# Decoder layer with mixture of experts: router logits as dot products on VectorE, experts split in order

## The reference, cut to what matters

```
x = x + self_attention(norm(x))              # causal, 16 heads of 32
x = x + cross_attention(norm(x), ctx)        # one head of 512; keys and values: 256 of ctx and 256 of norm(x) through wk, wv
x = x + ffn(norm(x))                         # 8 experts, top 1

ffn:  logits = xt @ wg                       # (2048 x 512) @ (512 x 8)
      probs = softmax(logits); idx = argmax(probs); gate = probs[idx]
      out = gate * (xt @ W[idx].T + b[idx])  # each expert's W is 512 x 512
```

## Time and profile before

| what | us |
|---|---|
| median of 3 runs | 755.86 (754.78 to 756.69) |
| profiled execution, its own time | 756.65 |
| its span, first to last instruction | 754.9 |
| TensorE busy in the span | 679.7 |
| VectorE busy | 502.1 |
| ScalarE, GpSimd busy | 309.3, 327.8 |
| mean granted TensorE clock | 0.963 |

### The profile page before, as it was taken

The page is one execution under the profiler, slowest core; times in us unless marked ns, Lnnn a source line. Parts: engine busy times, 40 slices in busy tenths (PEclk is TensorE's granted clock), DMA queues, the critical chain, the costliest instruction groups (busy, mean ns, idle before and its releaser), DMA issues.

```text
span 754.9 us, 18988 instructions
## 1 busy us (share of the span) xinstructions
PE 679.7 (90%) x6040; PEld 604.4 (80%) x6041; DVE 502.1 (67%) x1479; ACT 309.3 (41%) x985; POOL 327.8 (43%) x559
## 2 busy tenths in 40 slices
PE   4768999999999989899999999999999983779994
PEld 4658798989898878778899999989898973658883
DVE  4667788888887878754647474747474649665663
ACT  3445565656666666633132323232323344112220
POOL 4376757575756686823301010100101258345652
PEclk9889999999999999999999999999999997679997
DMA  6487875656556656837813434352422282676520
GB/s 250 136 166 117 131 148 111 149 116 145 137 124 142 124 124 124 185 61 252 296 53 105 59 102 63 98 68 87 80 83 56 78 173 57 224 139 198 167 98 14
DMA packets 142745, 95.10 MB, mean 126 GB/s; under 512 B 110702, under 2 KB 114926, under 8 KB 142576
## 3 DMA queue, kind: packets, MB, share of 16 engines
q1 hardware_dynamic: 137040, 82.00, 46.6%
q0 software_dynamic: 5664, 12.61, 6.1%
HBM read 56.14 MB, written 18.77 MB: 99 GB/s over the span
## 4 chain that ended last, share of the span: by engine, by line
PE 44%; DVE 4%; DMA 3%; POOL 2%; issue 1%; ACT 0%; SPq 0%; POOLq 0%; DVEq 0%
PE b_bank L61 38%; PE b_bank L1462 2%; PE b_bank L1410 2%; DMA stage<-x2n,k_gather_no 2%; DVE k_at L975 1%; PE b_bank L1787 1%; DMA bias_sb<-in_wo 1%; PE b_bank L1434 1%; POOL w_lo L1294 1%; DVE w_lo L1094 0%; POOL w_hi L1292 0%; DVE x_sb L1534 0%; DVE b_stats L1579 0%; DVE w_lo L1507 0%; POOL slots L889 0%
## 5 line engine op out<-in xcount | busy, mean ns | idle before, releaser
L509 ACT ACTIVATE prob<-prob,shift 128x128 f32<-128x128 f32 (+1 forms) x256 | 114.6, 449 | 116.5 <-POOL shift L420 116.1
L1337 ACT CAST w_hi<-b_bank 128x256 fp32r<-128x256 f32 (+1 forms) x128 | 55.0, 447 | 153.7 <-PE b_bank L61 133.1
L61 PE MATMUL b_bank<-w_hi 128*128 128x256 f32 (+1 forms) x528 | 106.5, 324 | 3.2 <-DVE w_lo L1507 3.2
L61 PE MATMUL a_job<-w_hi 128*128 128x256 f32 (+1 forms) x488 | 95.0, 318 | 15.5 <-DVE w_lo L712 7.2
L61 PE MATMUL b_bank<-w_lo,w_hi 128*128 128x256 f32 (+1 forms) x528 | 103.8, 319 | 0.0
L61 PE MATMUL b_bank<-w_hi,w_lo 128*128 128x256 f32 (+1 forms) x528 | 103.7, 319 | 0.0
L733 DVE CUSTOM_DVE_ANT_0 prob<-a_s,mask 128x128 f32<-128x128 f32 (+1 forms) x256 | 79.7, 347 | 30.1 <-PE a_s L609 30.0
L1507 DVE TENSOR_TENSOR w_lo<-b_bank,w_hi 128x256 fp32r<-128x256 f32 (+1 forms) x128 | 61.4, 510 | 47.9 <-ACT w_hi L1337 47.4
L61 PEld LDWEIGHTS a_job<-w_hi 128*128 128x128 f32 x488 | 71.7, 197 | 25.3 <-DVE w_lo L712 7.8
L61 PE MATMUL a_job<-w_lo,w_hi 128*128 128x256 f32 (+1 forms) x488 | 88.0, 304 | 0.0
L61 PEld LDWEIGHTS b_bank<-w_hi 128*128 128x128 f32 x528 | 80.3, 191 | 9.5 <-DVE w_lo L1507 3.6
(11 more groups left out here) (185 smaller groups left out, 1136.7 us busy)
## 6 DMA issues: line engine op xcount, KB each, us to landing
stage<-in_w SPq DMA_DIRECT2D x6, 1024.0 KB, 10.4
xin<-in_x SPq DMA_DIRECT2D x8, 512.0 KB, 4.3
xr<-in_x SPq DMA_DIRECT2D x8, 512.0 KB, 4.1
x<-xr SPq DMA_DIRECT2D x8, 512.0 KB, 3.2
xin<-x SPq DMA_DIRECT2D x8, 512.0 KB, 8.6
stage<-in_ctx_t SPq DMA_DIRECT2D x8, 512.0 KB, 3.6
stage<-in_ctx SPq DMA_DIRECT2D x8, 512.0 KB, 3.5
xr<-x SPq DMA_DIRECT2D x8, 512.0 KB, 4.4
```

What stands on the lines that cost most here:

```text
L61: ins = pe_matmul(out, a, b, start=first and i == 0, stop=last and i == len(steps) - 1)
L509: a = nc.scalar.activation(prob[:, e % NPROB, cols], prob[:, e % NPROB, cols], ACT.Exp, scale=-1.0, bias=shift[:, e, q:q + 1], accum_out=r ...
L1337: nc.scalar.copy(hi, src).then_inc(job_hi, 1)
```

## The change

The logits of batches 0 to 6 are no longer made by Y0, Y1, l0 and l1, which leave `ORDER` (22 jobs are left). VectorE computes each as a fused multiply and sum over 512 channels of a row of `xn3_sb` with a row of `wg_t`, the transposed router matrix, which a new input brings and one DMA copies to all partitions, into the bias's tile. There are 16 per batch (8 experts, 2 tiles of tokens), dealt out behind jobs by two tables: `DOTS` (7 behind k1 to v1, 9 behind X1 to q2 of the next batch) and, for batch 6, `LAST_DOTS` (all behind k1 to v1). The last batch keeps TensorE's way.

The banks: jobs 0 to 13 take the seven banks twice, jobs 14 to 21 the last four twice. `ctx_t_lo` moves from s1 to y0.

The experts are split in the order 0 to 7 with one semaphore, each waiting for the one before. The buffers are dealt anew (`BUFFER`), with `xin` and `xn` as a fifth buffer; the output rows of the products move to `xr` and `prob`. GpSimd splits 0, 1 and 2 only (2 ahead of `next_tokens`), VectorE the rest: 3 and half of 4 between o0 and o3, `known_blocks` behind o3, the rest of 4, and 5, by the norm's steps, half of 6 behind `choose`, and half of 6 and all of 7 in the first four blocks of the products. A product waits only for its own expert. SP's loads, and the bias in two halves, follow the new buffers. `gates` gets a semaphore of its own and stands behind `place_tokens` in the last batch's first half; `STEPS` is 8. Scratch places 6 and 7 change names.

```diff
-        done = n * self.STEPS
         dve.wait_ge(self.ex_done, n + 1)
-        nc.vector.tensor_reduce(self.gsum[:], self.ex[:], AX.X, ALU.add).then_inc(self.step, 1)
-        dve.wait_ge(self.step, done + 5)
+        nc.vector.tensor_reduce(self.gsum[:], self.ex[:], AX.X, ALU.add).then_inc(self.gsum_done, 1)
+        dve.wait_ge(self.gsum_done, n + 1)
...
+        dve.wait_ge(self.step, done + 7)
+        nc.vector.tensor_reduce(self.slot[:], self.place[:], AX.X, ALU.add).then_inc(self.step, 1)
         dve.wait_ge(self.step, done + 8)
-        nc.vector.tensor_reduce(self.slot[:], self.place[:], AX.X, ALU.add).then_inc(self.step, 1)
-        dve.wait_ge(self.step, done + 9)
+        dve.wait_ge(self.token_done, n + 1)
         nc.vector.tensor_copy(self.slot_i[:], self.slot[:]).then_inc(self.slot_done, 1)
...
-    BUFFER = (0, 1, 4, 3, 2, 0, 2, 1)
-    HIGH_ORDER = (0, 1, 2, 4, 3, 5, 7, 6)
+    BUFFER = (0, 1, 0, 1, 2, 3, 4, 2)
...
+    def parts(self, e):
+        parts = self.stage[self.BUFFER[e]]
+        size = DC // len(parts)
+        return [(part, slice(i * size, (i + 1) * size)) for i, part in enumerate(parts)]
 
     def load(self, sp, w, e):
-        b = self.BUFFER[e]
-        wait(sp, self.split[b], self.earlier(e) * DC)
-        sp.dma_start(self.stage[b], w[e].rearrange("(c p) n -> p c n", p=P)).then_inc(self.loaded[b], 16)
+        if self.earlier(e):
+            self.wait_split(sp, self.earlier(e)[-1])
+        for part, chunks in self.parts(e):
+            sp.dma_start(part, w[e][chunks.start * P:chunks.stop * P, :].rearrange("(c p) n -> p c n", p=P))\
+                .then_inc(self.loaded[self.BUFFER[e]], 16)
 
     def high(self, nc, act, e):
-        act.wait_ge(self.loaded[self.BUFFER[e]], 16 * (self.earlier(e) + 1))
-        nc.scalar.copy(self.place(e)[0], self.stage[self.BUFFER[e]]).then_inc(self.hi_done, 1)
+        loads = sum(len(self.parts(i)) for i in self.earlier(e) + [e])
+        act.wait_ge(self.loaded[self.BUFFER[e]], 16 * loads)
+        for part, chunks in self.parts(e):
+            m = nc.scalar.copy(self.place(e)[0][:, chunks, :], part)
+        m.then_inc(self.hi_done, 1)
 
     def low(self, engine, e, pieces=range(DC)):
         hi, lo = self.place(e)
-        b = self.BUFFER[e]
-        engine.wait_ge(self.hi_done, self.HIGH_ORDER.index(e) + 1)
+        engine.wait_ge(self.hi_done, e + 1)
+        if e and pieces[0] == 0:
+            self.wait_split(engine, e - 1)
         for c in pieces:
-            engine.tensor_tensor(lo[:, c, :], self.stage[b][:, c, :], hi[:, c, :].bitcast(F32), ALU.subtract)\
-                .then_inc(self.split[b], 1)
+            part, chunks = next(p for p in self.parts(e) if c in range(p[1].start, p[1].stop))
+            engine.tensor_tensor(lo[:, c, :], part[:, c - chunks.start, :], hi[:, c, :].bitcast(F32), ALU.subtract)\
+                .then_inc(self.split, 1)
 
     def wait_split(self, engine, e):
-        engine.wait_ge(self.split[self.BUFFER[e]], DC * (self.earlier(e) + 1))
+        engine.wait_ge(self.split, e * DC + DC)
...
-        ORDER = ("X0 X1 s0 s1 q0 q1 p0 p1 q2 q3 o0 o1 o2 o3 k0 y0 y1 k1 k2 k3 v0 Y0 Y1 v1 l0 l1").split()
+        ORDER = ("X0 X1 s0 s1 q0 q1 p0 p1 q2 q3 o0 o1 o2 o3 k0 y0 y1 k1 k2 k3 v0 v1").split()
         FRONT = "Xqkv"
+        DOTS = {"k1": 1, "k2": 1, "k3": 1, "v0": 2, "v1": 2, "+X1": 2, "+s0": 2, "+s1": 1, "+q0": 1, "+q1": 1, "+p1": 1,
+                "+q2": 1}
+        LAST_DOTS = {"k1": 2, "k2": 2, "k3": 2, "v0": 5, "v1": 5}
+        assert sum(DOTS.values()) == sum(LAST_DOTS.values()) == TB * E
+        def dots_behind(j, n):
+            whole = LAST_DOTS if isinstance(n, int) and n == B - 2 else DOTS
+            def part(dots, key):
+                first = sum(c for i, c in enumerate(dots.values()) if i < list(dots).index(key)) if key in dots else 0
+                return range(first, first + dots.get(key, 0))
+            return part(whole, j), part(DOTS, "+" + j) if has_routing(n) else ()
...
+        def number(j, n):
+            i = order(n).index(j)
+            return i % RING if order(n) is LAST or i < 2 * RING else RING - 4 + (i - 2 * RING) % 4
         def bank(j, n):
-            return ring[order(n).index(j) % RING]
+            return ring[number(j, n)]
...
+            def load_bias(i):
+                sp.dma_start(bias_sb[:, i * half:(i + 1) * half],
+                             bass.AP(tensor=bias.tensor, offset=bias.offset + i * half, ap=[[0, P], [1, half]]))\
+                    .then_inc(bias_in, 16)
...
-            for e in (0, 1, 2):
+            for e in (0, 1):
                 experts.load(sp, w, e)
             sp.wait_ge(wo_split, 2)
-            experts.load(sp, w, 3)
+            sp.dma_start(bias_sb[:], bass.AP(tensor=wg_t.tensor, offset=wg_t.offset, ap=[[0, P], [1, E * D]]))\
+                .then_inc(wg_all_in, 16)
...
-            experts.load(sp, w, 4)
+            for e in (4, 2):
+                experts.load(sp, w, e)
+            sp.wait_ge(job_ev, ev_at("X1", B - 2))
+            experts.load(sp, w, 6)
             batch(B - 2, True, False)
-            for e in (5, 7, 6):
-                experts.load(sp, w, e)
+            experts.load(sp, w, 3)
+            sp.wait_ge(dots_done, (B - 1) * TB * E)
+            experts.load(sp, w, 5)
+            load_bias(1)
+            experts.load(sp, w, 7)
             sp.wait_ge(blocks.known_done, 2)
             sp.wait_ge(routing.entries_in, 16 * TB * (B - 1))
             for k in range(Blocks.KNOWN):
                 blocks.entries(sp, routing.table, 0, k)
-            for e in (2, 3):
-                experts.wait_split(sp, e)
-            sp.dma_start(bias_sb[:], bass.AP(tensor=bias.tensor, offset=bias.offset, ap=[[0, P], [1, E * D]]))\
-                .then_inc(bias_in, 16)
+            experts.wait_split(sp, 5)
+            load_bias(0)
...
+            experts.low(nc.gpsimd, 2)
             routing.next_tokens(nc, pool, tick_pool, B - 3)
-            experts.low(nc.gpsimd, 2)
             routing.store_entries(nc, pool, tick_pool, B - 2)
-            for e in (4, 3):
-                experts.low(nc.gpsimd, e)
...
-        FREE = {("q3", B - 2): (0,), ("k3", B - 2): (1,), ("v1", B - 2): (2,), ("p1", B - 1): (4, 3), ("o3", B - 1): (5, 7)}
+        FREE = {("q3", B - 2): (0,), ("k3", B - 2): (1,), ("v1", B - 2): (2,), ("p1", B - 1): (3, 4), ("o3", B - 1): (5, 6)}
...
+            def dot(i, n):
+                e, t = divmod(i, TB)
+                if i == 0 and isinstance(n, int) and n == 0:
+                    dve.wait_ge(wg_all_in, 16)
+                if i == 0:
+                    dve.wait_ge(xn3_ready, (n + 1) * TB)
+                    dve.sem_inc(tick, 1)
+                if i >= 2 or has_routing(n):
+                    dve.wait_ge(dots_done, n * TB * E + i - 1)
+                    dve.sem_inc(tick, 1)
+                nc.vector.tensor_tensor_reduce(out=unwanted[:, i % 2, :], in0=xn3_sb[:, t, :], in1=wg_all[:, e, :], scale=1.0,
+                                               scalar=0.0, op0=ALU.mult, op1=ALU.add,
+                                               accum_out=routing.logits[:, t, e:e + 1]).then_inc(dots_done, 1)
...
+                        dve.wait_ge(dots_done, n * TB * E)
                         dve.sem_inc(tick, 1)
                         routing.choose(nc, dve, n - 1)
                         routing.gates(nc, dve, n - 1)
+                    if j == "k1":
+                        wait(dve, xn3_out, 16 * n)
+                        dve.wait_ge(ln3_rstd, n + 1)
+                        norm_apply(1, xn3_sb, x2_sb, xn3_ready)
+                    own, before = dots_behind(j, n)
+                    for i in own:
+                        dot(i, n)
+                    for i in before:
+                        dot(i, n - 1)
                     if j == "k0" and has_routing(n):
                         routing.place_tokens(nc, dve, n - 1)
-                    if j == "s1":
+                    if j == "y0":
...
             def last_batch(n):
 
-                dve.wait_ge(job_ev, ev_at("l1", n - 1))
+                dve.wait_ge(dots_done, n * TB * E)
                 dve.sem_inc(tick, 1)
                 routing.choose(nc, dve, n - 1)
                 scores_max("s0", n)
                 scores_max("s1", n)
-                routing.gates(nc, dve, n - 1)
                 lo_part("p0", n)
                 lo_part("p1", n)
                 routing.place_tokens(nc, dve, n - 1)
+                routing.gates(nc, dve, n - 1)
                 nc.vector.reciprocal(rinv[:], rsum[:]).then_inc(rinv_done, 1)
+                lo_part("o0", n)
+                experts.low(nc.vector, 3, (0, 1))
+                lo_part("o1", n)
+                experts.low(nc.vector, 3, (2, 3))
+                lo_part("o2", n)
+                experts.low(nc.vector, 4, (0, 1))
+                lo_part("o3", n)
                 blocks.known_blocks(nc, dve, routing)
```

(43 more changed lines are left out.)

59 lines of the change are left out of this document (27 added, 32 removed).

## The result

The changed kernel takes 752.70 us (median of 6 runs, 751.91 to 753.37), the kernel before 755.29 (6 runs, 754.32 to 756.69): ratio 0.9957, 95% interval 0.9939 to 0.9974. It is faster, but by 2.6 us and not by the 14.4 forecast, and 752.7 lies above the range of 734 to 750. The profiled execution has a span of 751.0 us (before 754.9).

What follows compares the result with a forecast made beforehand. TensorE was taken to bound the loop, and waits the later stretches. Gains of 14.1 us in batches 0 to 5 and 1.2 in the tail, 15.3 together, gave 741.4 from the profiled 756.65, forecast as 741.5; range 734 to 750.

Steps and rivals of the forecast that it cites:

- the bounds of 0.5 and 1.2: Loop, VectorE: limits in us set for one 512-wide dot product, with 0.61 taken from start to start.
- Rivals 1: Loop: VectorE becomes the bound if a dot takes over 1.1 us, kernel slower, 768 us at 1.2; chance 5%.
- 4: Loop and tail: TensorE waits 1.5 us or more per turn and the tail is poor, 753 to 757; chance 6%.
- Rival 3: Tail: port conflicts stay small, o0 at 50, fifth block at 95 to 96, 735 us; chance 22%.
- the old stall: Last batch: TensorE's 12.60 us wait ahead of y0 would go, and no 10 us operation would remain on VectorE.
- I take 101.5, a gain of 1.2: Tail: fifth gathered block's transposes start 101.5 us behind X0 of batch 6, before 102.7; ends 96 and 109.
- I take 5 of the 9: Batch 6: dots serialized with GpSimd's splits of experts 1 and 2 end up to 9 us later; 5 assumed, o0 at 55.
- the bound of 60: Sign of being wrong: o0 of the last batch more than 60 us behind X0 of batch 6.
- The 2 us taken beside the split of expert 0: Batch 6: VectorE's choice of experts slowed beside GpSimd's split, 0 to 5 us; 2 assumed on TensorE.
- The 10.34 us row: Earlier trace: a small VectorE operation lasted 10.34 us beside all eight GpSimd pieces; counted against putting dots there.
- 9 + 1.2: Tail: expert 7 split 9 us after the first product, plus 1.2 for two quarters, before the fifth block's gather.
- Rival 2: Tail eats its gain: dots serialized with both splits (4 more), fifth block late (5 more), 750 us; chance 20%.

Runs made afterwards that it cites:

- experiment 5: Changed kernel with the subtraction of the context's low part (`ctx_t_lo`) back at s1 instead of y0: 759.33 us, ratio 1.0056 to the kernel before.
- experiment 6: Changed kernel with all 22 jobs taking the seven banks in plain turn: 760.46 us, ratio 1.0073 to the kernel before.
- experiment 2: Changed kernel with GpSimd's split pieces of experts 1 and 2 cut to 8 of 512 columns: 750.10 us, ratio 0.9896 to the kernel before.
- experiment 7: Changed kernel with expert 2's low part subtracted by VectorE instead of GpSimd: 748.98 us, ratio 0.9929 to the kernel before.
- experiment 3: Changed kernel with GpSimd computing the second tile's norm factor ahead of the first gather: 752.72 us, ratio 0.9925 to the kernel before.
- experiment 4: Changed kernel with SP asking for the table ahead of expert 7's load: 748.25 us, ratio 0.9871 to the kernel before.
- Experiment 8: Changed kernel with the table requested ahead of expert 7's load and all expert 7 quarters split in the products' second block: 745.03 us, ratio 0.9854.

## Why the prediction was wrong

**Right: the loop.** Forecast 36.0 us a turn with VectorE near 30.5 and a wait of 0.3 at o0; measured 36.19, 30.2 to 30.6, and 0.32, at that place. A dot lasts 0.68 us (median of 112) and follows the next at 0.61, as taken from the earlier trace rows and the subtractions of the earlier trace rows; the bounds of 0.5 and 1.2 were not needed. A turn gained 2.08 and not 2.3, five turns 10.4. The first transposes of batch 0 lie 0.4 us earlier than before, and batch 0 is 3.9 shorter, 1.3 of it at an early TensorE wait for VectorE (1.76, now 0.44) that is anything from 0.4 to 1.8 in the runs here. Together 14.3 us, where 14.1 stood. But the 1.3 us of that early wait are luck: without them it is 13.0, because a turn gave 2.08 and not 2.3. Rivals 1 and 4 fall with their condition, a slow turn (that 4's range of 753 to 757 begins beside the measured 752.7 is no support for its mechanism). Rival 3 falls with o0 at 57.9 instead of 50.

**Right: the conditions.** Undoing the move or the dealing of banks costs 6.6 and 7.8 us (experiments 5 and 6).

**Right: the old stall.** The wait of 12.60 us and the operation of 10.34 are gone; the same operation, now at L976, takes 0.21. The clock does not halve at y0 either: granted 1.00 from 627.9 to 634.0, before 0.50 in the first 2.4 us of y0.

**Wrong: the tail.** The step that failed is the sum for it, "I take 101.5, a gain of 1.2". Measured is 112.5, 11.0 later, in four parts:

- *The dots beside both splits, 2.9 of the 11.0.* Forecast "I take 5 of the 9", o0 at 55; the dots were 7.7 late and o0 came at 57.9, still inside the bound of 60. The forecast named its 9 and took about half without a row for that. Experiments 2 and 7 show the cause. The 2 us taken beside the split of expert 0 were too many: three operations of the choice lasted 1.30, 1.22 and 1.01 us there instead of 0.17, but TensorE reached k0 only 0.5 us later than in a turn without that split (19.9 behind X0, else 19.4). The 10.34 us row did not repeat: beside the pieces of experts 1 and 2 no dot waited for more than one piece. The Trainium skill (SBUF — State Buffer, SBUF: two separate sides) says that of a VectorE operation with two SBUF inputs and a GpSimd operation that reads SBUF, the one that starts first holds the shared port pair for its whole instruction while the other is blocked. These rows, at most one piece per dot, agree.
- *o0 to y0, 1.2.* 9.7 us instead of 8 to 9, the first six product groups at the halved clock (granted 0.50 from 618.2 to 623.4; 1.19 and 1.05 us instead of 0.64 to 0.71). It had fallen in the waits ahead of them, and not only because they hold 10.49 us: in experiment 2, where that wait is 2.83, o0 starts at 0.50 as well. That the clock alone made the 1.2 us is not shown.
- *y0 to the first product, 4.9.* Forecast 22.0, measured 26.9. The prediction had written that SP asks for the table only behind expert 7's load, and that this waits for expert 4's last quarter near 70 (measured 74.4, about as late as y0). It took "a few us" for the table and stopped there. It landed at 80.3, and the forecast did not ask who else stood behind it: GpSimd's factor for the second tile is queued behind the gather that waits for it. Through that factor l0 waits 5.94 us, and block 0 moves to 89.9, beyond the 80 to 84. Without the factor's wait (experiment 3) it would still be at 86.2, behind its own gather. Experiments 3 and 4 show it; the table's request in its old place costs 3.9 to 6.5 us at the end.
- *First product to fifth block, 2.0.* The mechanism is the one forecast, a gather waiting for expert 7; the size was off. Its last quarter ended 12.3 us behind the first product's start, not 9 + 1.2: the fourth block's subtraction stands behind a product at the halved clock (2.07 us for four) and the planning of the other blocks on VectorE. Experiment 8 shows that the gather's wait for expert 7 costs 1.3 to 4.0 at the end; how the 2.0 are shared between clock and planning is not shown.

The end lies 1.0 us further behind the fifth block. Less 0.6 in which the start was better, 11.0 + 1.0 - 0.6 = 11.4: the profiled 751.0 against 739.6 (754.9 less 15.3). Taken off the median of 755.86, as the forecast is a median, the 15.3 would have given 740.6 and not 741.5, a little further off still.

**How the chances stood.** Rival 2, the tail eating its gain, is what happened, with both causes as named: the dots serialized with both splits, and the fifth block late. It was given 20% and 750; it lacked the table's chain. Several errors with the same sign in one chain made more than the bound of any one, and the range added only two of them.

Left open: how much of the tail the halved clock costs by itself. No run here changed it alone.

## What to carry to other kernels

When work moves off the bounding engine, walk the stage behind the loop queue by queue: for each waiting instruction list what stands behind it on its own engine and on the DMA queue, then who waits for those. A request whose data are ready (the table) must not stand behind a load that waits for a buffer. When an unknown has two ends and no row between them, take the end that the mechanism gives, not the middle, and add the late ends of one chain together in the range.
